# First feed-forward of a four-layer kernel: statistics ahead of all else, one power for all scores, weights scaled by ScalarE and VectorE, biases added later, the heavy expert's result taken from PSUM by halves

## The reference, cut to what matters

```
x = x + tanh(g_ffn[0]) * ffn(layernorm(x))

def ffn(x, token, light..., heavy...):
    light_out = gelu(rms_norm(x, light_gamma) @ w1l + b1l) @ w2l + b2l      # hidden 128
    s = einsum('bnd,d->bn', x, token)
    scores = coor_descent(s, k=288, n_iters=50, eps=1.0)                    # 50 rounds of logsumexp and relu
    sel = top 256 of each sequence by scores
    heavy_out = gelu(rms_norm(x[sel], heavy_gamma) @ w1h + b1h) @ w2h + b2h # hidden 1024
    return light_out + heavy_out placed at sel
```

## Time and profile before

| | us |
|---|---|
| median of 3 runs (lowest, highest) | 3290.38 (3288.73, 3294.31) |
| the execution that was profiled | 3289.11 |
| its span | 3287.4 |

### The profile page before, as it was taken

How to read it: one execution, slowest core, us unless ns; L and a number is a source line. 1 busy time by engine, 2 the same in 40 slices (tenths; PEclk the granted TensorE clock), 3 DMA queues, 4 the chain that set the end, 5 groups by cost and what they waited for, 6 DMA issues and landing times. The chain is left out here.

```text
span 3287.4 us, 41337 instructions
## 1 busy us (share of the span) xinstructions
PE 2956.4 (90%) x15957; PEld 1581.2 (48%) x15973; DVE 1659.4 (50%) x3305; ACT 1291.2 (39%) x1784; POOL 1299.5 (40%) x1038
## 2 busy tenths in 40 slices
PE   7889899999999999686889999978888899998798
PEld 3456334434434344244458889843333223322587
DVE  4535555564455455466662112147553877776400
ACT  4432444344343434346521111124333465565232
POOL 2241366565666556610235222214555210000433
PEclk9999999999999999897999999989998999999899
DMA  1400100000000000000006455520001000000376
GB/s 54 123 17 1 38 6 5 11 5 6 5 10 6 5 6 1 26 0 28 1 30 235 168 214 199 209 83 6 1 14 36 1 1 1 1 1 1 123 242 173
DMA packets 72758, 172.03 MB, mean 52 GB/s; under 512 B 17501, under 2 KB 52242, under 8 KB 59764
## 3 DMA queue, kind: packets, MB, share of 16 engines
q0 software_dynamic: 21744, 118.63, 10.5%
q1 hardware_dynamic: 50820, 50.75, 4.9%
HBM read 142.23 MB, written 27.64 MB: 52 GB/s over the span
## 5 line engine op out<-in xcount | busy, mean ns | idle before, releaser
L1520 POOL TENSOR_TENSOR l1x_added<-l1x_added,l1x_probs 128x1024 f32<-128x1024 f32 x224 | 527.2, 2354 | 264.9 <-ACT l1x_probs L1791 198.6
L1888 DVE TENSOR_REDUCE l1x_tops<-l1x_ring 128x1 f32<-128x512 f32 x512 | 326.8, 686 | 192.9 <-PE l1x_ring L1600 192.6
L1121 DVE TENSOR_REDUCE l3a_halves<-l3a_ring 128x1 f32<-128x512 f32 x512 | 325.0, 684 | 99.6 <-PE l3a_ring L966 95.4
L1791 ACT ACTIVATE l1x_probs<-l1x_slots 128x1024 f32<-128x1024 f32 x256 | 261.7, 1024 | 238.9 <-PE l1x_slots L1644 237.1
L1637 PE MATMUL l1x_slots<-l1x_Q,l1x_K 64*128 64x512 f32 x1152 | 309.5, 615 | 6.0 <-ACT l1x_probs L1789 4.8
L1082 ACT ACTIVATE l3a_probs<-l3a_slots 128x1024 f32<-128x1024 f32 x256 | 248.2, 1021 | 160.6 <-PE l3a_slots L986 160.6
L1659 PE MATMUL l1x_pv<-l1x_probs,l1x_V 128*64 128x512 f32 x1152 | 284.4, 610 | 0.0
L986 PE MATMUL l3a_slots<-l3a_Q,l3a_K 32*128 32x512 f32 x1024 | 150.2, 637 | 35.5 <-ACT l3a_probs L1082 34.7
L3439 DVE TENSOR_TENSOR l2f_hh<-l2f_sg,l2f_hid 128x256 f32<-128x256 f32 (+1 forms) x184 | 69.9, 381 | 214.2 <-ACT l2f_sg L3286 214.2
L3286 ACT ACTIVATE l2f_sg<-l2f_hid 128x256 f32<-128x256 f32 (+1 forms) x184 | 64.5, 351 | 282.6 <-PE l2f_hid L3202 280.4
L3202 PE MATMUL l2f_hid<-l2f_xgT,l2f_gate 128*128 128x256 f32 (+1 forms) x736 | 167.7, 351 | 3.1 <-ACT l2f_xgT L3273 2.4
(11 more groups left out here) (706 smaller groups left out, 5192.8 us busy)
## 6 DMA issues: line engine op xcount, KB each, us to landing
l1x_w<-in_l_qkv SPq DMA_DIRECT2D x16, 384.0 KB, 3.1
slots_in<-zeros SPq DMA_DIRECT2D x1, 4992.0 KB, 18.2
l2f_yg<-rows_out SPq DMA_DIRECT2D x8, 512.0 KB, 5.6
l2f_xg<-slots_in SPq DMA_DIRECT2D x15, 272.0 KB, 3.6
slots_in<-zeros SPq DMA_DIRECT2D x1, 2944.0 KB, 19.3
x<-in_x SPq DMA_DIRECT2D x4, 512.0 KB, 7.9
l1f_w<-in_l_w SPq DMA_DIRECT2D x2, 1024.0 KB, 7.0
x<-x SPq DMA_DIRECT2D x4, 512.0 KB, 2.9
```

Of the source, the lines that this page charges most:

```text
L1121: nc.vector.tensor_reduce(halves[:, k % 2, col:col + 1], bank_of(banks[e]), AX.X, ALU.max).then_inc(s["bank_done"], 1)
L1520: ins = nc.gpsimd.tensor_tensor(added[h][:], added[h][:], probs[:, n % PROBS, :, :], ALU.add)
L1791: ins = nc.scalar.activation(p, s2[m % 2], ACT.Exp)
L1888: ins = nc.vector.tensor_reduce(tops[:, e * NT + t, h:h + 1], bank, AX.X, ALU.max)
```

## The change

In the list of events, the statistics of all chunks (a new event "stats", on DVE) come first; ("busy", n) is new, n products of constants into a PSUM bank that nothing has written yet. The norms, dots and turns are put closer together, with fewer steps of bulk work between them: 12 instead of 16 stand ahead of centre 0, and two instead of four between "final" and "rows", so that 98 steps instead of 104 stand ahead of "rows". The scores' factor is computed once for all 16 tiles (`rates`): one power over 128x16 and floor * size in place of a second power. ACT scales the light weights (`scale_light`, after norm 1), DVE the heavy ones (`scale_heavy`, after dot 0), POOL none. b2l is added to x only after the exponential of centre 0 (`add_biases`). Gelu's table is asked for at the stage's start. The heavy result is copied and gets its bias in halves of two tiles, and `close` waits for halves. w1h is loaded before b1.

```diff
-    plan = [("norm", 0), ("norm", 1), ("turn", 0), ("dot", 0)]
+    plan = [("stats", n) for n in range(NC)]
+    plan += [("norm", 0), ("busy", 24), ("norm", 1), ("turn", 0), ("dot", 0), ("busy", 8)]
...
-    work(3)
-    plan.extend([("norm", 2), ("turn", 1), ("dot", 1)])
+    plan.append(("norm", 2))
+    work(2)
+    plan += [("norm", 3), ("turn", 1), ("rates",)]
+    work(2)
+    plan += [("dot", 1), ("dot", 2), ("dot", 3), ("turn", 2)]
     work(4)
-    plan.extend([("norm", 3), ("turn", 2), ("dot", 2)])
-    work(4)
-    plan.extend([("turn", 3), ("dot", 3)])
-    work(3)
+    plan.append(("turn", 3))
+    work(2)
     plan.append(("best",))
     work(2)
     plan.append(("spread",))
...
     plan.append(("final",))
-    work(4)
+    work(2)
     plan.append(("rows",))
...
             def norm(n):
-                var = mv[:, n, :, 1]
                 pool.wait_ge(s["var_ready"], n + 1)
-                step.add(pool.tensor_scalar(floor[:, n, :], var, TINY, None, ALU.max))
-                step.add(pool.tensor_scalar(ratio[:, n, :], var, EPS, None, ALU.add))
+                step.add(pool.tensor_scalar(floor[:, n, :], mv[:, n, :, 1], TINY, None, ALU.max))
...
-                step.add(pool.tensor_tensor(ratio[:, n, :], ratio[:, n, :], down[:], ALU.pow))
-                step.add(pool.tensor_tensor(floor[:, n, :], floor[:, n, :], up[:], ALU.pow))
+
+            def rates():
+                step.add(pool.tensor_scalar(ratio[:], mv[:, :, :, 1], EPS, None, ALU.add))
+                step.add(pool.tensor_tensor(floor[:], floor[:], size[:], ALU.mult))
                 step.wait()
...
-                for k in range(KD):
-                    pool.tensor_scalar(w1l[:, k, :], w1l[:, k, :], gam[:, k, 0:1], None, ALU.mult).then_inc(s["w1_scaled"], 1)
-                    pool.tensor_scalar(w1h[:, k, :], w1h[:, k, :], gam[:, k, 1:2], None, ALU.mult).then_inc(s["w1_scaled"], 1)
+                step.add(pool.tensor_tensor(ratio[:], ratio[:], down[:], ALU.pow))
+                step.wait()
+                pool.tensor_tensor(ratio[:], ratio[:], floor[:], ALU.mult).then_inc(s["ratio_ready"], 1)
...
+            def add_biases():
+                pool.wait_ge(s["xn_ready"], NC)
+                pool.wait_ge(s["ex_ready"], 1)
                 for n in range(NC):
                     chunk = x[:, n * CT:(n + 1) * CT, :]
-                    pool.wait_ge(s["xn_ready"], n + 1)
...
+            def keep_busy(n):
+                for _ in range(n):
+                    nc.tensor.matmul(hid[:, 1, 0:P], c.ident[:], c.ones[:], start=True, stop=True)
...
-                        pe.wait_ge(s["w1_scaled"], 4)
+                        pe.wait_ge(s["w1l_scaled"], KD)
+                    if n == 0 and i == 1:
+                        pe.wait_ge(s["w1h_scaled"], KD)
...
-                if t == CT - 1 and k == MH - 2:
+                if t % 2 and k == MH - 2:
                     last.then_inc(s["heavy_psum"], 1)
...
+            def scale_light():
+                act.wait_ge(s["gam_loaded"], 16)
+                act.wait_ge(s["w1l_loaded"], 16)
+                for k in range(KD):
+                    nc.scalar.activation(w1l[:, k, :], w1l[:, k, :], ACT.Copy, scale=gam[:, k, 0:1]).then_inc(s["w1l_scaled"], 1)
...
+            def scale_heavy():
+                dve.wait_ge(s["gam_loaded"], 16)
+                dve.wait_ge(s["w1h_loaded"], 16)
+                for k in range(KD):
+                    nc.vector.tensor_scalar(w1h[:, k, :], w1h[:, k, :], gam[:, k, 1:2], None, ALU.mult).then_inc(s["w1h_scaled"], 1)
```

More of the change, by code:

```diff
@@ L2063, in ffn0 @@
         size, lean, ratio = sb("size", [P, NC, CT]), sb("lean", [P, NC, CT]), sb("ratio", [P, NC, CT])
-        floor, down, up = sb("floor", [P, NC, CT]), sb("down", [P, CT]), sb("up", [P, CT])
+        floor, down, up = sb("floor", [P, NC, CT]), sb("down", [P, NC, CT]), sb("up", [P, B])
         tok, gam = sb("tok", [P, D]), sb("gam", [P, KD, 2])
@@ L2112, in norm @@
             def norm(n):
-                var = mv[:, n, :, 1]
                 pool.wait_ge(s["var_ready"], n + 1)
-                step.add(pool.tensor_scalar(floor[:, n, :], var, TINY, None, ALU.max))
-                step.add(pool.tensor_scalar(ratio[:, n, :], var, EPS, None, ALU.add))
+                step.add(pool.tensor_scalar(floor[:, n, :], mv[:, n, :, 1], TINY, None, ALU.max))
                 step.wait()
-                step.add(pool.tensor_tensor(size[:, n, :], floor[:, n, :], down[:], ALU.pow))
+                step.add(pool.tensor_tensor(size[:, n, :], floor[:, n, :], down[:, n, :], ALU.pow))
                 step.wait()
@@ L2157, in light, with heavy @@
                 pool.tensor_tensor(chunk, chunk, yl[n % 2][:], ALU.add).then_inc(s["light_added"], 1)
[L2159 to L2162, removed]
+            def heavy(n, i):
+                part = yh[:, n * CT + 2 * i:n * CT + 2 * i + 2, :]
+                pool.wait_ge(s["heavy_kept"], 2 * n + i + 1)
+                pool.tensor_tensor(part, part, b2h[:].unsqueeze(1).broadcast_to([P, 2, D]), ALU.add).then_inc(s["heavy_added"], 1)
             for e in plan:
@@ L2166, in _ @@
                     norm(e[1])
-                    if e[1] == 1:
-                        scale_weights()
-                elif e[0] == "dot" and e[1] == 3:
+                elif e[0] == "rates":
+                    rates()
                     set_rest()
+                elif e[0] == "centre" and e[1] == 0:
+                    add_biases()
                 elif e[0] == "light":
                     light(e[1])
-                elif e[0] == "heavy" and e[2:] == (CT - 1, MH - 2):
-                    heavy(e[1])
+                elif e[0] == "heavy" and e[2] % 2 and e[3] == MH - 2:
+                    heavy(e[1], e[2] // 2)
                 elif e[0] == "centre" and e[1]:
@@ L2246, in _ @@
             for e in plan:
-                if e[0] == "turn":
+                if e[0] == "busy":
+                    keep_busy(e[1])
+                elif e[0] == "turn":
                     turn(e[1])
@@ L2291, in light, with heavy @@
                                      scale=gate_col).then_inc(s["light_kept"], 1)
-            def heavy(n):
-                act.wait_ge(s["heavy_psum"], n + 1)
-                nc.scalar.activation(yh[:, n * CT:(n + 1) * CT, :].rearrange("p t d -> p (t d)"), out[:].rearrange("p t d -> p (t d)"), ACT.Copy,
+            def heavy(n, i):
+                act.wait_ge(s["heavy_psum"], 2 * n + i + 1)
+                part = yh[:, n * CT + 2 * i:n * CT + 2 * i + 2, :]
+                nc.scalar.activation(part.rearrange("p t d -> p (t d)"), out[:, 2 * i:2 * i + 2, :].rearrange("p t d -> p (t d)"), ACT.Copy,
                                      scale=gate_col).then_inc(s["heavy_kept"], 1)
@@ L2315, in _ @@
                     normalise(e[1])
+                    if e[1] == 1:
+                        scale_light()
                 elif e[0] == "turn":
@@ L2452, in _ @@
             for e in plan:
-                if e[0] == "norm":
+                if e[0] == "stats":
                     norm(e[1])
@@ L2456, in _ @@
                     dot(e[1])
+                    if e[1] == 0:
+                        scale_heavy()
                 elif e[0] == "best":
```

28 lines of the change are left out of this document (13 added, 15 removed).

## The result

| | before | after |
|---|---|---|
| median of 4 runs (lowest, highest) | 3292.35 (3288.73, 3294.58) | 3270.94 (3267.95, 3274.70) |
| the profiled execution, and its span | 3289.11, 3287.4 | 3273.44, 3271.7 |

The ratio of after to before is 0.9936, with a 95% interval of 0.9921 to 0.9952. The forecast of 3272.5 and its range of 3267 to 3279 hold the median.

A forecast was written before the change was run, and what follows sets the result against it. PE's pace bounds the stage from 200 to 293 us, waits on POOL its opening, DVE its end. PE's 16.0 lead less 2.8 and 0.3, with the shorter end, gives 16.9 saved: 3272.5 us, range 3267 to 3279.

The forecast's parts named there:

- The opening: Stage start: first hidden product at 167.4 instead of 176.45, 9.1 us earlier; PE 16.0 us ahead at equal work.
- the four causes in the check: PE's lead in the opening: 9.1 of the wait, 2.1 half clock, 1.1 Gelu wait, 3.2 before the maximum, making 15.5.
- The clock: PE in the opening: full clock throughout, with a gap of 2.4 us before the filler and later ones under 1.
- The rival had feared: Opening gives less: low clock at 157.8 loses 6.8 us (3279), or 1 to 2 if it recovers; chance 0.18.
- Additions at centre 0: First round of centre 0: DVE's SBUF-only instruction may wait for POOL's b2l addition; PE waits 0.6 or 0, taken as 0.3.
- The waits at the centres: Centres 1 and 2: PE waits for ACT's Gelu behind yl's copy and table load, two stalls of 1.4, 2.8 in all.
- The rival without waits: No stall at the centres: ACT's chain is shorter, 2.8 come back, stage ends at 311.0, total 3269.5; chance 0.20.
- The end: Stage end: PE's last product at 310.9, half copies and updates to 313.9; DVE's own path ends at 310.5.
- some 3: Sign at the stage's end: DVE waits some 3 us for the two half copies behind PE's last product.
- The power over 128x16: POOL's single power for the rates: between 1.04 and 4.2 us, middle taken, costing nothing with 2.7 us of cover.

The follow-up runs named there:

- powers_back: Changed kernel with the scores' factor made in each norm again by two more POOL powers, ahead of the next norm's statistics; stage 161.33 us against 155.23.
- weights_pool: Changed kernel with POOL scaling both light and heavy weights again, behind norm 1; stage 161.74 us against 155.23.
- powers_back_filled: Changed kernel with two more POOL powers in each norm again, and 20 filler products in place of the second 8; stage 161.35 us against 155.23.
- bias_early: Changed kernel with each chunk's b2l addition following as soon as its xn is made, as before the change; stage 157.64 us against 155.23.
- light_after_6: Changed kernel with the light output products behind hidden slice 6 instead of 5; stage 153.22 us against 155.23, total 3270.36 us.
- heavy_whole: Changed kernel with the heavy result copied, given its bias and waited for in one piece per chunk again; stage 157.65 us against 155.23.
- no_busy: Changed kernel without the 24 and 8 filler products of constants; stage 156.71 us against 155.23.

## Why the prediction was right, step by step

**The opening.** Forecast: 9.1 us earlier for the first hidden product, and 16.0 at equal work. Measured from S: 8.93 (18.64 to 9.71), and 15.75 (43.38 to 27.63). Of the four causes in the check (the wait, the half clock, a Gelu, the maximum) none shows in the opening after. `powers_back` and `weights_pool` confirm the reading that POOL's queue was what held ACT, and they show more than the text said. The prediction priced the scaling mostly as PE's wait for the weights; the 6.5 and 6.1 us come through ACT's later normalisations, behind either kind of work on POOL. How far the two losses add up isn't shown, as no kernel here has both in the new opening. POOL does the two kinds one behind the other: it has chunk 3's `lean` ready at 10.83 from S in the changed kernel (169.21), at 18.99 in `powers_back` (179.85), at 18.79 in `weights_pool` (176.73), and at 25.31 before (183.12), where both stand in its queue. That they make up most of the 15.75 is likely from this, but argued. The statistics' place, the table load at the stage's start and the order of the loads were not taken back one by one. The statistics' old place cost nothing before: POOL, once it had started at 159.80, waited for none.

**The clock.** The sum had it full throughout, and so it was in this profile. But the reading that the gap of 2.4 us leaves the clock full held in seven of ten executions only. The ten executions with filler (the changed kernel, its repeat and eight edits) have the 24 products behind a gap of 2.37: seven took 5.60 for them and three 7.22. A gap of 3.17 kept the clock in one place and lost it in `weights_pool`. The Trainium skill (TensorE: Matmul & The Clock Gate, why this matters for your kernels) wants no gap above about 3 us; the rows on the 2.37 and 2.77 us gaps disagree with it in one direction and those on the 3.17 us gap of before in the other; the 3.17 us gap of `weights_pool` agrees. In the changed kernel the slower 24 products would have cost little, by an estimate from the rows: chunk 0's transposes come 7.06 behind their start (166.51 and 159.45 in `powers_back_filled`) instead of 6.14, 0.92 later; the eight products behind them then end at 168.3 instead of 167.4, 0.2 behind the 168.09 at which the hidden products start. The rival had feared 1 to 2, or 6.8.

**Additions at centre 0: 0.3 expected, 0 measured.** DVE's instruction was 0.07 us ahead of POOL's and took 0.18. The mechanism itself is there: `bias_early` shows it at 1.30 to 2.27 on instructions of a few elements. The Trainium skill (SBUF — State Buffer, who interferes with whom) says that GpSimd issuing first blocks a DVE instruction with two SBUF inputs, and that a tensor_scalar, though it has one input, can use the shared ports too. The rows agree with both: 1.64 is an instruction with two inputs, 1.30 and 2.27 are TENSOR_SCALARs.

**The waits at the centres: 2.8 expected, 2.08 measured.** The mechanism was right and the size off by a quarter. The Gelu's end was set at 7.86 and PE's arrival at 6.55 behind the last round's product; with that product at 216.31 PE came to the wait at 6.75 (223.06, the end of the round at 222.78), and stood until 7.79 (224.10). So PE came 0.2 later than summed and went on 0.16 earlier, part of it because yl's copy begins beside the exponential's tail (220.95 against 221.04). `light_after_6` showed the cause by removing it. The rival without waits had the stage end at 311.0, 153.2 from S; `light_after_6` comes to 153.22.

**The end.** Forecast: PE's last product at 310.9, which is 153.1 from S, and 3.0 behind it. (The stage's gain follows as 330.70 less 313.9, 16.8, where the forecast wrote 16.9.) Measured: 152.26 and 2.97 (155.23). DVE waited 3.57 for "some 3". The 0.8 at PE's end is, but for 0.1, the two terms above (0.7 of the waits, 0.3 of the additions) less 0.25 of the opening. The stretch behind PE's end shrank from 6.89 to 2.97. `heavy_whole` gives the halves 2.42 of these 3.9; the rest is that before the change DVE's own path ended the stage, and not PE's last product: its last eight updates followed its ranking without a wait.

**The power over 128x16** took 3.21, inside the bounds of 1.04 and 4.2, and was covered: DVE's maximum was ready at 174.72 and PE came to it at 179.38.

**The total.** The stage gained 17.66; the span 15.7 and the profiled execution's own time 15.67, because the later stages' starts scatter against each other by 1 to 3 us (the second layer's attention starts 17.1 earlier, the third layer's feed-forward 13.6). The medians differ by 21.4 and by 19.7, more than the stage gives; the intervals, 0.9921 to 0.9952 and 0.9922 to 0.9949, hold 17.66 us (0.9946), and also the 0.993 that the rival had, a further gain in later stages. That the rest is scatter of the stage ahead is likely, given the 9 us between executions, and the profiled pair shows no further gain behind this stage, but it is not shown for the medians.

## What to carry to other kernels

Follow an engine that is rarely busy by its queue, not by its share: two tiny powers per chunk and a weight scaling on POOL each held the whole opening by over 6 us, through ACT. Before a lower clock, a wait or a filler is given a price, ask what the engine waits for next: twice some 1.7 us of lower clock lay entirely ahead of a wait for another engine, and filling the gap moved the stage by 0.02 us at most, while the same kind of filler where PE was itself the path was worth 1.5. Around a change of activation table, put copies that any table can do behind the load back, if a product waits for the function.

## What the runs showed of the hardware

**A gap's length alone doesn't decide the clock.** The same gap of 2.37 us ahead of the same products kept the clock in seven executions and lost it in three; 2.77 lost it in `powers_back`; 3.17 kept it before 198.78 and lost it in `weights_pool`. What else decides is open. Where it had fallen, it was back 3.0 us after the products began in `no_busy`; in `powers_back` it was 0.50 from 161 to 164, behind products that began at 160.82.

**A tiny DVE instruction can wait out a long POOL instruction.** Beside POOL's 128x1024 additions of 2.35 us a 2x2 DVE instruction took 1.30 and 128x2 ones 1.64 and 2.27, where they take 0.22, 0.16 and 0.17 without it.

**POOL's power grows less than its columns.** 128x4 took 1.04 and 128x16 3.21 (2.99 in `weights_pool`). Four small ones would be 4.2, so joining them saves 1.0 us of POOL. The rates took eight before, 8.3 by this figure; the other four are saved because a multiplication of 0.33 takes their place. The gain of 6.1 us for the stage (`powers_back`) is more than this time, as the power now stands behind all four `lean`s for which ACT waits.
